# Transposes set two by two behind the score passes, and a third PSUM bank for the middle slots

## What is computed

```python
q, k, v = jnp.einsum('bsx,xMnd->Mbnsd', x, qkv)
a = jnp.einsum('bnsd,bntd->bnst', q, k) * q.shape[-1] ** (-0.5)
bias = jnp.where(rel >= 0, cum[:, jnp.clip(rel, 0)], PAD)
a = jax.nn.softmax(a + bias, axis=-1)
mix = jnp.einsum('bnst,bntd->bnsd', a, v)
x = layernorm(x + jnp.einsum('bnsd,ndx->bsx', mix, out_w))
# then: r = sigmoid(xr @ W_r); k = relu(xk @ W_k)**2; x = layernorm(x + r * (k @ W_v))
```

## Time and profile before

| | |
|---|---|
| time, median of 3 runs | 1121.46 us (1121.15 to 1122.28) |
| the profiled execution | 1119.69 us, of which the span of instructions is 1118.0 us |
| granted TensorE clock over the span | 0.989 of full speed |
| PE busy | 1064.6 us (95%) |
| DVE busy | 806.7 us (72%) |
| ACT busy | 731.7 us (65%) |
| DMA, mean share of the 16 engines | 162 GB/s; largest queue 63.5% |

### The profile page before, as it was taken

One profiled execution on the slowest core, in us unless ns is written; L12 is line 12 of the kernel. 1 busy time (PEld: TensorE's weight loads), 2 busy tenths in 40 slices (PEclk: granted clock), 3 DMA queues, 4 the chain that ended last, 5 costly groups with the idle time before them and its releaser, 6 DMA issues.

```text
span 1118.0 us, 21664 instructions
## 1 busy us (share of the span) xinstructions
PE 1064.6 (95%) x6975; PEld 754.0 (67%) x6975; DVE 806.7 (72%) x2129; ACT 731.7 (65%) x1870; POOL 5.4 (0%) x15
## 2 busy tenths in 40 slices
PE   5899999999999999999999999999999999999994
PEld 3666666765666776666776676777676677666774
DVE  2766566776667788777788777778877778877766
ACT  2666666765767676666676676777676767666643
POOL 1000000000000000000000000000000000000000
PEclk8899999999999999999999999999999999999997
DMA  7756767666666767567667666677756766765810
GB/s 174 163 159 161 181 167 173 156 157 159 160 158 170 182 152 182 156 156 186 170 161 180 164 156 166 161 176 176 183 152 162 168 172 156 186 157 151 242 55 21
DMA packets 116222, 180.72 MB, mean 162 GB/s; under 512 B 13680, under 2 KB 72960, under 8 KB 116112
## 3 DMA queue, kind: packets, MB, share of 16 engines
q1 hardware_dynamic: 112992, 176.85, 63.5%
q10 hardware_dynamic: 3120, 2.49, 0.9%
HBM read 58.41 MB, written 20.22 MB: 70 GB/s over the span
## 4 chain that ended last, share of the span: by engine, by line
PE 68%; DVE 5%; issue 5%; ACT 4%; DMA 2%; SPq 2%; DVEq 0%
PE ps_o L1081 20%; PE ps_rows L1040 18%; PE ps_t L1057 10%; PE ps_m L1015 7%; PE ps_m L1020 4%; PE ps_m L1097 4%; PE ps_o L1057 2%; ACT prob L542 2%; DVE pt L742 2%; DMA stacks<-k_lo 1%; SPq L314 1%; ACT pt L558 1%; DVE prob L720 1%; PE ps_rows L1136 1%; PE ps_t L1062 1%
## 5 line engine op out<-in xcount | busy, mean ns | idle before, releaser
L542 ACT ACTIVATE prob<-prob,low 128x128 f32<-128x128 f32 (+7 forms) x512 | 395.6, 774 | 109.5 <-DVE low L720 104.3
L720 DVE CUSTOM_DVE_ANT_0 prob<-ps_rows,table 128x128 f32<-128x128 f32 (+7 forms) x512 | 379.8, 750 | 44.6 <-PE ps_rows L1040 28.2
L1040 PE MATMUL ps_rows<-stacks 128*128 128x512 f32 (+3 forms) x1536 | 395.6, 369 | 10.0 <-issue 6.5
L1057 PE MATMUL ps_t<-ident_r,prob_r 128*128 128x128 f32 x1984 | 283.8, 262 | 11.3 <-ACT pt L558 4.6
L1057 PEld LDWEIGHTS ps_t<-ident_r,prob_r 128*128 128x128 f32 x1984 | 211.9, 141 | 95.7 <-issue 72.8
L1081 PE MATMUL ps_o<-pt,v_pair 128*64 128x512 f32 (+3 forms) x1536 | 268.9, 492 | 0.0
L1040 PEld LDWEIGHTS ps_rows<-stacks 128*128 128x128 f32 x1536 | 246.0, 190 | 31.5 <-issue 6.6
L742 DVE COPY pt<-ps_t 128x256 f32<-128x256 f32 (+2 forms) x320 | 178.1, 565 | 115.2 <-PE ps_t L1057 114.9
L1081 PEld LDWEIGHTS ps_o<-pt,v_pair 128*64 128x64 f32 x1536 | 101.6, 136 | 175.8 <-issue 163.5
L558 ACT ACTIVATE pt<-ps_t 128x512 f32<-128x512 f32 (+3 forms) x352 | 163.1, 463 | 81.6 <-PE ps_t L1057 81.1
L1015 PE MATMUL ps_m<-x_cur,w_cur 128*128 128x512 f32 x250 | 131.2, 606 | 4.2 <-ACT x_t L511 2.2
(11 more groups left out here) (127 smaller groups left out, 605.3 us busy)
## 6 DMA issues: line engine op xcount, KB each, us to landing
stacks<-k_hi SPq DMA_DIRECT2D x124, 256.0 KB, 4.5
stacks<-k_lo SPq DMA_DIRECT2D x124, 256.0 KB, 5.0
inv_all<-inverse_sums SPq DMA_DIRECT2D x128, 128.0 KB, 3.4
stacks<-q_hi SPq DMA_DIRECT2D x62, 256.0 KB, 4.0
stacks<-q_lo SPq DMA_DIRECT2D x62, 256.0 KB, 4.4
mix_transposed<-mix_sb SPq DMA_DIRECT2D x62, 256.0 KB, 3.6
table<-bias_by_distance SPq DMA_DIRECT2D x64, 192.0 KB, 3.8
mix_tile<-mix_transposed SPq DMA_DIRECT2D x24, 448.0 KB, 3.9
```

The costliest lines, as they stand in the source:

```text
L542: nc.scalar.activation(row, row, ACT.Exp, bias=low[:, r:r + 1], scale=-1.0, accum_out=total[:, r:r + 1]).then_inc(s_exp, 1)
L720: nc.vector.tensor_tensor_reduce(prob[:, r % PSLOTS, 0:width], ps_rows[:, score_at(r):score_at(r) + width], table[n % 2][:, h, 0:width][:, ...
L1040: ins = nc.tensor.matmul(ps_rows[:, at + c0:at + c1], q_st(h, n)[:, P * i:P * i + P], k_st(h, n, low_part)[:, c0:c1], start=(low_part == 0 ...
L1057: ins = nc.tensor.transpose(t_bank[TBANK[k]][:, P * b:P * b + P].bitcast(F32R), prob_r[:, r % PSLOTS, at:at + P], ident_r[:, :])
```

## The change

**The order on PE.** `score` is cut into its single passes, and `transpose` into its single blocks. In the six slots of `AMONG` (3, 6, 7, 10, 11, 15) up to two blocks of the slot's row are transposed behind every score pass of exactly 512 columns; the blocks that are left come where all of them stood. In slots 3, 7 and 11 none is left. In slot 11 the eight transposes so move from behind the mix to ahead of it.

**The banks.** `TBANK` now gives bank 2 (`ps_o`) also to k9 and k12, between the store of the far mix in slot 6 and the near mix in slot 11, and from k16 on to k18 and k21. k9 and k18, the first behind a mix, wait for the mix's store (`BEHIND_MIX`); the near mix waits for the copy of k12.

**DVE's slot 11.** The copy of k15 comes ahead of the gate's reciprocal, the gated product and the store of the mix; it stood behind them.

**Types.** The transposes of `inv` and `x1` are done as F32R, like those of `prob`: 64 and 23 matmuls in all.

```diff
-TBANK = [k % 2 for k in range(16)] + [2, 0, 1, 2, 0, 1, 2, 1]
+TBANK = [0, 1] * 4 + [0, 2, 1, 0, 2, 1, 0, 1] + [0, 1, 2, 0, 1, 2, 0, 1]
+BEHIND_MIX = (9, 18)
...
+AMONG = (3, 6, 7, 10, 11, 15)
...
-                    if tile_too and slot == V_PROJ:
-                        tile_step(n, GATE)
-                        tile_step(n, V_PROJ)
-                    if slot == MIX_NEAR:
-                        store_mix(n, 0)
                     if slot in INV_READY:
                         invert(n, INV_READY.index(slot))
...
                     if slot != LATE_SLOT:
                         empty_banks(n, slot)
+                    if tile_too and slot == V_PROJ:
+                        tile_step(n, GATE)
+                        tile_step(n, V_PROJ)
+                    if slot == MIX_NEAR:
+                        store_mix(n, 0)
...
+            def passes(r):
+
+                at, width = score_at(r), P * (ROWS[r][1] + 1)
+                cut = min(BANK - at % BANK, width)
+                return [(c0, max(c1, c0 + SHORTEST), low_part) for c0, c1 in ((0, cut), (cut, width)) if c0 < c1
+                        for low_part in range(2)]
...
+            def transpose(n, r, block, tile_too):
...
+                if block == 0:
+                    pe.wait_ge(s_exp, NROWS * n + r + 1)
+                if block == b0:
+
+                    if k in BEHIND_MIX:
+                        pe.wait_ge(s_o, 2 * n + 1 + BEHIND_MIX.index(k))
                     else:
                         engine, count = emptied(n, k)
                         pe.wait_ge(s_ev[engine], count)
...
                         last_bank = max(k for k in range(NBANKS) if ROWS[BANKS[k][0]][1] < GROUP * (g + 1))
+                        if g == 0:
+                            last_bank = max(k for k in range(BEHIND_MIX[1]) if TBANK[k] == 2)
...
-                    for row in rows_ahead(n, more, slot):
-                        score(*row)
+                    blocks = ROWS[slot][1] + 1
+                    moved = 0
+                    for m, row in rows_ahead(n, more, slot):
+                        for which in range(len(passes(row))):
+                            score(m, row, which)
+                            c0, c1, _ = passes(row)[which]
+                            share = min(2, blocks - moved) if slot in AMONG and c1 - c0 == BANK else 0
+                            for block in range(moved, moved + share):
+                                transpose(n, slot, block, tile_too)
+                            moved += share
...
-                    transpose(n, slot, tile_too)
+                    for block in range(moved, blocks):
+                        transpose(n, slot, block, tile_too)
```

More of the change, by code:

```diff
@@ L124, in build @@
         prob = sb("prob", [P, PSLOTS, SEQ])
+        with nc.sbuf_tensor("inv_r", [P, NROWS], F32R) as inv_r:
+            pass
+        inv = sb("inv", [P, NROWS])
+        with nc.sbuf_tensor("x1_r", [P, C], F32R) as x1_r:
+            pass
+        x1 = sb("x1", [P, C])
         ident = sb("ident", [P, P])
@@ L140, in build @@
         total = sb("total", [P, NROWS])
-        inv = sb("inv", [P, NROWS])
         inv_t = [sb(f"inv_t{g}", [2 * GROUP, P]) for g in range(2)]
@@ L150, in build @@
         o_tile = sb("o_tile", [P, C])
-        x1 = sb("x1", [P, C])
         x1_t = sb("x1_t", [P, 1 + SEQ])
@@ L1022, in project @@
                 ins.then_inc(s_proj, 1)
-            def score(n, r):
-                h, i = ROWS[r]
[L1027 to L1051, removed]
+            def passes(r):
[3 more added lines that the diff above has]
+                        for low_part in range(2)]
@@ new lines, in score @@
+            def score(n, r, which):
+                h, i = ROWS[r]
+                if which == 0:
+                    if n == 0 and i == 0:
+                        pe.wait_ge(s_first[h], 96)
+                    elif i % GROUP == 0:
+                        pe.wait_ge(s_stack[h], 96 * n + 96)
+                    pe.wait_ge(s_biased, NROWS * n + r + 3 - rows_since(r))
+                c0, c1, low_part = passes(r)[which]
+                at = score_at(r)
+                ins = nc.tensor.matmul(ps_rows[:, at + c0:at + c1], q_st(h, n)[:, P * i:P * i + P],
+                                       k_st(h, n, low_part)[:, c0:c1], start=(low_part == 0), stop=(low_part == 1))
+                if which == len(passes(r)) - 1:
+                    ins.then_inc(s_score, 1)
@@ L1052, in transpose @@
+            def transpose(n, r, block, tile_too):
+                k = next(k for k in range(NBANKS) if BANKS[k][0] == r and BANKS[k][1] == block // 4 * 4)
+                _, b0, nb = BANKS[k]
+                bank = t_bank[TBANK[k]].bitcast(F32R)
+                if block == 0:
[3 more added lines that the diff above has]
+                        pe.wait_ge(s_o, 2 * n + 1 + BEHIND_MIX.index(k))
                     else:
@@ L1054, in transpose @@
                         pe.wait_ge(s_ev[engine], count)
[L1055 to L1058, removed]
+                ins = nc.tensor.transpose(bank[:, P * (block - b0):P * (block - b0) + P],
+                                          prob_r[:, r % PSLOTS, P * block:P * block + P], ident_r[:, :])
+                if block == b0 + nb - 1:
                     if k in INV_BANK:
@@ L1061, in transpose @@
                         pe.wait_ge(s_inv, 2 * n + g + 1)
-                        ins = nc.tensor.transpose(t_bank[TBANK[k]][0:2 * GROUP, 3 * P:],
-                                                  inv[:, 2 * GROUP * g:2 * GROUP * (g + 1)], ident[:, :])
+                        ins = nc.tensor.transpose(bank[0:2 * GROUP, 3 * P:],
+                                                  inv_r[:, 2 * GROUP * g:2 * GROUP * (g + 1)], ident_r[:, :])
                     if k == X1_BANK and tile_too:
                         pe.wait_ge(s_chain, CH * (n - TILE_LAG + 1) + 4)
-                        ins = nc.tensor.transpose(t_bank[TBANK[k]][:, P:2 * P], x1[:, :], ident[:, :])
+                        ins = nc.tensor.transpose(bank[:, P:2 * P], x1_r[:, :], ident_r[:, :])
                     ins.then_inc(s_tr, 1)
@@ L1115, in _ @@
             for r in range(LEAD):
-                score(0, r)
+                for which in range(len(passes(r))):
+                    score(0, r, which)
             pe.wait_ge(s_in_w, 64)
```

## The result

| | before | after |
|---|---|---|
| time, median of 4 runs each | 1121.78 us (1121.15 to 1122.28) | **1154.04 us** (1151.34 to 1156.23) |
| profiled execution, and its span | 1119.69, 1118.0 us | 1154.05, 1152.3 us |
| granted TensorE clock | 0.989 | 0.987 |

The ratio is 1.0285 (95% interval 1.0268 to 1.0303). The forecast was 1143 us with a range of 1128 to 1149: the sign was right, the size was two thirds of what came.

A forecast was written before the change was run, and what follows sets the result against it. PE was taken to bound the step up to the end of row 10's scores, DVE the rest. 0.81 us in 23 steps with tile work (18.6) and 0.30 in 9 without (2.7) gave +21.3 us: 1143 us, range 1128 to 1149.

The forecast's parts named there:

- What bounds the kernel: A step is PE-bound from k19 to the end of row 10's scores (19.07 us), then 13.96 us set by DVE.
- Pairs between passes: Transposes between score passes on PE: a pair costs 0.12 + 0.07 = 0.19 us, the 0.07 on the pass behind.
- The rival in which the pass behind a pair doesn't pay: On PE the 0.07 us of the score pass behind a pair vanish: +7 us, 1128; chance 0.07.
- Slot 6: Row 6's three transposes now precede row 10's 384-column passes: those scores and DVE's stretch come 0.32 us later.
- Slots 7 to 10: k9's wait of 0.33 us goes, but row 13's scores wait for row 11's bias: gain costed at nothing.
- Slots 10 and 11: Row 15's scores end 0.61 us later, 0.17 comes back before k15's copy: k19 starts 0.44 us later.
- Slots 12 to 5 of the next step (PE-bound): Pairs in slots 15 and 3 cost only their splits, +0.05 and +0.03 us; k21's wait goes, -0.03.
- The copy's new place changes no sum: DVE, slot 11: with k15's copy moved, the same instructions stand between row 15's bias and k16's copy.
- PE-bound: Rival: PE is the bound after all and freed waits go for good: -0.59 us a step, 1102; chance 0.10.
- slack: Rival: the delays meet unseen slack; only 0.25 us of further runs or less remain, 1122 to 1129; chance 0.08.
- half: Rival: DVE's stretch absorbs one of two delays; a step gains 0.3 to 0.5 us, some 1134; chance 0.15.

The follow-up runs named there:

- the kernel before with DVE relieved: Kernel before, with the gate's reciprocal ahead of row 15's bias and k6 and k15 copied by ACT, not DVE: 1123.51 us, ratio 1.0.

## Why the prediction was right in sign and short in size

**What bounds the kernel: right for this change.** The loop of DVE in slots 6 to 12 and PE in the rest carries every measured term. DVE isn't alone in its stretch, though: the kernel before with DVE relieved gets no shorter step (33.25), because the copies behind the mix come late there. Taking work off DVE pays once slot 11's transposes stand ahead of the mix.

**Pairs between passes: right.** 0.13 and 0.30 us in the rows of after. The rival in which the pass behind a pair doesn't pay is out; the Trainium skill's rule behind it (TensorE: Matmul & The Clock Gate, "What happens when you issue a matmul": weight loads are pulled ahead of running matmuls) is borne out here for the pair and not for the pass behind it.

**Slot 6: right.** 0.30 in the trace, and 0.30 given back when it was taken out.

**Slots 7 to 10: right for the changed kernel.** The gain is taken back by row 13's scores. But "at nothing" hides that the table costs 0.35 us where slot 11 keeps its old order, and there the mix does wait for the copy of k12, 0.14 us, which the prediction called free.

**Slots 10 and 11: right in mechanism.** Row 15's bias is 0.64 later behind row 10's scores, not 0.61. The return is larger. An instruction that follows one of 0.69 us without a break starts 0.60 us behind its start (694.68 to 695.28), since the rows overlap; before, the copy started 0.87 behind the store (675.49 to 676.36 in the earlier trace rows). So 0.27 goes, not 0.17: 0.64 - 0.27 = 0.37, measured 0.35.

**"Slots 12 to 5 of the next step (PE-bound)": the step that failed.** It costed the pairs of slots 15 and 3 as splits, 0.08 us, on the ground that PE does the same work in another order. It did not ask what stands behind the moved transposes on PE and who waits for that. In both slots it is a projection into the single bank `ps_m`, which ACT (slot 15's) or ACT and then DVE (slot 3's) must empty before PE's next work in it. Before, these copies ended 0.15 and 0.31 us ahead of that work; the pairs used this up. The waits and what follows them are 0.54 us a step with tile work and 0.63 without: 23 x 0.54 + 9 x 0.63 = 18.1 us. The step lengths put the whole at 37.7 us where the forecast had 21.3, and these 18.1 are more than that difference of 16.4; the terms of slots 6 to 12 give 2 us back. The medians lie 32.3 us apart, 5.4 less than the product, so that the forecast ended 11 us short and not 16.

**"The copy's new place changes no sum": right as it stood,** with slot 11's transposes ahead of the mix. Without them it cost 58 us over the banks alone (1189.5 in a single run, against 1131.1), part of it by the clock.

**PE-bound, slack and half: out.** None of the delays that the forecast named was absorbed.

## What to carry to other kernels

When work is moved ahead of something in an in-order queue, list every instruction that it passes, find the consumer of each on the other engines and what is released by that consumer: here two pairs ahead of a projection cost 0.34 us by the work behind it, and 0.05 by their splits. A reordering that frees an engine's input can be worth nothing while another engine in the loop is full, and room there can be worth nothing while the input comes late: here slot 11's reordering alone cost 0.4%, the relief of DVE tried here gave nothing by itself, and both together gave 1.2%. The pairs of the other five slots cost 2.2% on top of it, so a table of slots like this one is worth trying entry by entry.

## What the runs showed of the hardware

A stall of PE can cost more than its own length: in the kernel with the copy of k15 ahead and no pairs, with PE busy for 4.33 of 5.88 us, the granted clock fell to 1.2 GHz for the next 6.4 us. Over the run the clock there was 0.964 where the changed kernel had 0.987, which is 27 us of full-speed time ((0.987 - 0.964) x 1187.8). The changed kernel's waits of 0.2 to 0.6 us left it at full speed in both windows shown of it. F32R or f32 made no difference for the 87 transposes of `inv` and `x1` (ratio 0.9994, 0.9982 to 1.0006).
